# Tail of a perceiver block: output weights loaded a step sooner, query weights in four loads, products of queries and keys in four banks, and filled gaps on TensorE

## The chip, the core and the metric

The kernel runs on one NeuronCore of a Trainium2 chip. The metric is the device time of one execution in microseconds, taken as the median of several. A core has five engines that run their own instruction streams and wait for each other by semaphores: TensorE (PE), VectorE (DVE), ScalarE (ACT), GpSimd (POOL) and SyncE (SP), which here issues every transfer.

## The reference

One block over x (128 rows of 512) and a context of 12544 rows of 512, all in float32:

```
x = x + cross(layernorm(x), context)   # 16 heads of 32; q, k rms-normed; image part 257 keys, text part the rest; two softmaxes
x = x + attn(layernorm(x))             # 16 heads of 128; wq, wk, wv: 512 x 2048, wo: 2048 x 512, each codes * scales per 32 rows
x = x + moe(layernorm(x))              # 32 experts (512 -> 256 -> 512, silu gate), top 4 of 32 in 2 of 4 groups, plus a shared expert
```

## The kernel before

**Main part (to about 910 us).** The context is worked through in groups of 512 keys (`GK`), one step `s` of the loop a group, NG groups in all. In a step TensorE makes keys and values of one group, scores and softmax products of the group before it, and closes the sums of the one before that. Beside it GpSimd multiplies the codes of the self-attention weights with their scales, and SyncE passes them through a DRAM buffer called `scaled`. The step ends in a drain without new keys (s = NG, NG + 1).

**Tail.** It has these stages, all with 128 rows on the partitions:

1. `last_values`: the last products with values. ACT copies them out of PSUM (`store_attention`, L888 to L892, tile `ot_sb`), TensorE transposes, DVE scales and adds (L1296, L1298).
2. Output projection of the cross attention (PE L1814): four 128x512 products of `xnt` (shown as `kb`, copied by ACT at L988 and L990) with `wo`. DVE adds x (L1399), takes mean and variance, centers (L1079, `yn`).
3. The self attention's projections. Each of q, k and v has four column blocks of 512 (index i = 0 to 11). The product is split for precision: a high part of the weights (`weight_hi`, made by ACT, `self_high`, L984), a low part (`weight_lo`, made in place by DVE, `self_low`, L1392) and high and low parts of the input (`ynt_hi`, `ynt_lo`). One block on TensorE is 12 products of 128x512: L1829, L1832, L1836, four each. DVE adds the bias (`add_bias`, L1411) and so frees the PSUM bank. Before, all twelve blocks share two banks (`ps_pj`).
4. Transposes of q and k, scores, softmax, values (L1851, L1017, L1436, L1865), then the output projection with `weight_o` (L1893, 32 instructions). DVE adds `bo_row` to x (L1420) ahead of the bias of the first value block and ahead of the maxima of the scores.
5. DVE adds (L1453) and centers; TensorE transposes; router logits (PE L1904); 34 experts (two halves of the shared one and 32), each with an `up` product (L1916, L1919, L1922), silu on ACT (L1055), gate on DVE (L1501), two transposes and a `down` product. Weights of an expert are split on ACT (L1034, L1040) and DVE (L1441, L1447).

**What sets the order.** Every engine's order is the order in which the program issues. Transfers of the tail are issued by SyncE in the order of the code after `steps(eng, step)`: query weights (4 MB), `wo` (1 MB), the two biases (each 1 MB when spread over 128 partitions), key weights, value weights, value bias, `weight_o`, `bo_row`, gate, experts. The semaphores: `e_pj` counts finished projection blocks, `e_pjb` biased ones, `e_shi` and `e_slo` high and low parts of weights, `e_ap` the output projection of the cross attention.

The first high part (i = 0) was written into 184 KB of the on-chip memory. `wo` lies at 144 KB, where the context tile `cx` lies during the main part.

Of the kernel before, what the change touches and what calls it, by code (L numbers as in the profile page):

```python
# [10 lines left out]
P = 128  # L11
D = 512
# [30 lines left out]
def program(nc, t, out):  # L43
    ctx = ExitStack()
    with ctx:
# [93 lines left out]
        NWH = 3  # L139
        weight_hi = [sb(f"weight_hi{i}", at * KB, [P, DC, D], F32R) for i, at in enumerate((184, 128, 144))]  # L140

        sq = sb("sq", 152 * KB, [P, SF])
# [96 lines left out]
        e_cm = semaphore("codes_scaled")  # L239
        e_wl = {n: semaphore(f"weight_loaded_{n}") for n in QKV + "o"}  # L240
        e_bias = {n: semaphore(f"bias_loaded_{n}") for n in QKV}
# [90 lines left out]
        def self_block(array, i):  # L332

            return array[QKV[i // NB]][:, :, :].rearrange("p (c b) f -> p b c f", b=NB)[:, i % NB]

        N_POOL = 2 + 2 + 2 + 1 + 1 + 2 + 4

# [7 lines left out]
        def _(eng):  # L345
# [52 lines left out]
            def step(eng, s, m, loop=False):  # L398
# [22 lines left out]
                if s == 0:  # L421
                    load_next(s)
                    eng.wait_ge(e_klo, GT)
                    eng.wait_ge(e_vp, GT)
                    stack(0, True)
                if 1 <= s < NG:
                    load_next(s)
                    eng.wait_ge(e_klo, s * GT + GT)
                    if score:
                        eng.wait_ge(e_qk, s * NH - NH // 2)  # L430
                    stack(0, False)
# [12 lines left out]
            eng.wait_ge(e_pp, 2 * (NG - 1) * NPOS)  # L444
            load_matrix("q")
            eng.dma_start(wo[:, :, :], wview(t["o_wt"])).then_inc(e_wo, 16)
            load_bias("q")
            load_bias("k")
            eng.wait_ge(e_kt, NG * GT)
            eng.wait_ge(e_v, NG * GT)  # L450
            eng.wait_ge(e_pv, (NG - 1) * (NH // HC))
            load_matrix("k")
            eng.wait_ge(e_qk, NG * NH)
            load_matrix("v")
            eng.wait_ge(e_pv, NG * (NH // HC))
            load_bias("v")
            eng.wait_ge(e_x1, 1)
            load_matrix("o")
# [256 lines left out]
        def _(eng):  # L715
# [113 lines left out]
            def step(eng, s, m, loop=False):  # L829
# [146 lines left out]
            def self_high(i):  # L976

                if i % NB == 0:
                    eng.wait_ge(e_wl[QKV[i // NB]], 16)
                if i == NWH - 1:  # L980
                    eng.wait_ge(e_ap, 1)
                elif i >= NWH:
                    eng.wait_ge(e_pj, i + 1 - NWH)
                eng.activation(weight_hi[i % NWH][:, :, :], self_block(weight, i), copy).then_inc(e_shi, 1)  # L984

            self_high(0)
            eng.wait_ge(e_at, 1)
# [76 lines left out]
        def _(eng):  # L1064
# [324 lines left out]
            def self_low(i):  # L1389

                eng.wait_ge(e_shi, i + 1)
                eng.tensor_tensor(self_block(weight_lo, i), self_block(weight, i), weight_hi[i % NWH][:, :, :].bitcast(F32),  # L1392
                                  ALU.subtract).then_inc(e_slo, 1)

            self_low(0)
            self_low(1)
            eng.wait_ge(e_xb, 1)
# [4 lines left out]

            center(yn[:, :], x1[:, :])

            def add_bias(n, b):
# [4 lines left out]
                eng.wait_ge(e_rs, 3)  # L1410
                eng.scalar_tensor_tensor(part, ps_pj[b % 2][:, :], rstd, part, ALU.mult, ALU.add).then_inc(e_pjb, 1)  # L1411
# [105 lines left out]
        def _(eng):  # L1517
# [298 lines left out]


            eng.wait_ge(e_ln, 1)
            transposes(ps_t, yn).then_inc(e_lnt, 1)
            eng.wait_ge(e_lntc, 1)  # L1820

            def project(n, b):
                i = QKV.index(n) * NB + b
                high, low = weight_hi[i % NWH], self_block(weight_lo, i)
                if i >= 2:
                    eng.wait_ge(e_pjb, i - 1)
                eng.wait_ge(e_shi, i + 1)
                for c in range(DC):
                    eng.matmul(ps_pj[b % 2][:, :], ynt_hi[:, c * P:(c + 1) * P], high[:, c, :], start=(c == 0), stop=False)  # L1829
                eng.wait_ge(e_slo, i + 1)  # L1830
                for c in range(DC):
                    eng.matmul(ps_pj[b % 2][:, :], ynt_hi[:, c * P:(c + 1) * P], low[:, c, :], start=False, stop=False)  # L1832
                if i == 0:
                    eng.wait_ge(e_ylo, 1)
                for c in range(DC):
                    last = eng.matmul(ps_pj[b % 2][:, :], ynt_lo[:, c * P:(c + 1) * P], high[:, c, :], start=False, stop=(c == DC - 1))  # L1836
                last.then_inc(e_pj, 1)
# [57 lines left out]


            eng.wait_ge(e_ln, 2)
            transposes(ps_t, x3).then_inc(e_lnt, 1)
# [102 lines left out]
```

## Time and profile before

| | us |
|---|---|
| median of 3 runs | 1187.23 (1186.8 to 1187.3) |
| profiled execution, its own time | 1185.77 |
| its span, first to last instruction | 1184.0 |
| mean granted TensorE clock | 0.993 of full speed |
| PE busy / DVE busy / ACT busy / POOL busy | 1149.0 / 970.4 / 874.6 / 761.1 |

The span is what the trace shows; 1.8 us lie around it. Times in the trace count from the span's start. "Busy" is the time in which an engine executes at least one instruction, waits not counted. Each waiting instruction has in brackets how long its engine stood idle and what released it.

### The profile page before, as it was taken

How to read it: one execution, taken by the hardware profiler on the slowest of the kernel's cores; microseconds unless marked ns; L12 is line 12 of the kernel's file. 1: busy time of each engine (PE TensorE's matmuls, PEld its weight loads, DVE VectorE, ACT ScalarE, POOL GpSimd, SP SyncE). 2: the span in 40 equal slices, each digit the busy share in tenths (PEclk: the TensorE clock that was granted, in tenths of full speed). 3: DMA queues.
4: the chain of work that ended last, by engine and by line, in shares of the span. 5: the costliest groups of instructions: out<-in, count | busy, mean ns of one | idle time of the engine just before them, and what ended most of it. 6: DMA issues, size and time to landing. Idle time of an engine off the chain costs nothing.

```text
span 1184.0 us, 26319 instructions
## 1 busy us (share of the span) xinstructions
PE 1149.0 (97%) x8794; PEld 948.5 (80%) x8794; DVE 970.4 (82%) x1601; ACT 874.6 (74%) x1890; POOL 761.1 (64%) x1064
## 2 busy tenths in 40 slices
PE   6899999999999999999999999999999879999998
PEld 4778888888888888888888888888887658588886
DVE  4778888888888888888888888888887878499997
ACT  5577777778777777777777777877777756387786
POOL 6998889888888888898888988888872200000000
PEclk9999999999999999999999999999999989899999
DMA  7135776666766667766677665677655899589990
GB/s 248 46 89 140 202 194 167 182 175 177 197 179 173 186 161 198 189 178 181 167 202 193 170 180 173 178 197 179 182 144 120 257 395 398 208 300 356 367 359 12
DMA packets 129327, 236.72 MB, mean 200 GB/s; under 512 B 15014, under 2 KB 42150, under 8 KB 128812
## 3 DMA queue, kind: packets, MB, share of 16 engines
q1 hardware_dynamic: 129196, 235.05, 67.1%
q8 instruction: 73, 1.20, 0.4%
q14 instruction: 58, 0.48, 0.1%
HBM read 140.87 MB, written 17.04 MB: 133 GB/s over the span
## 4 chain that ended last, share of the span: by engine, by line
PE 91%; DMA 2%; POOL 2%; SPq 2%; DVE 1%; ACT 1%; issue 1%; DVEq 0%; ACTq 0%; POOLq 0%
PE ps L1657 39%; PE ps L1521 19%; PE ps L1684 7%; PE ps L1714 7%; PE ps L1916 3%; PE ps L1919 3%; PE ps L1922 3%; DMA wo<-o_wt 1%; SPq L361 1%; PE ps L1937 1%; PE ps L1945 1%; PE ps L1941 1%; PE ps L1893 1%; PE ps L1832 1%; PE ps L1836 1%; PE ps L1829 1%
## 5 line engine op out<-in xcount | busy, mean ns | idle before, releaser
L1657 PE MATMUL ps<-w_text,cx_blocks 128*128 128x512 f32 x1974 | 488.2, 394 | 0.5 <-ACT v_first L827 0.5
L1657 PEld LDWEIGHTS ps<-w_text,cx_blocks 128*128 128x128 f32 x1974 | 366.9, 188 | 87.0 <-issue 9.4
L873 ACT ACTIVATE p<-ps,small 128x512 f32<-128x512 f32 (+2 forms) x400 | 272.2, 681 | 142.2 <-DVE small L1234 134.7
L1232 DVE TENSOR_REDUCE small<-ps 128x1 f32<-128x512 f32 (+2 forms) x384 | 258.8, 674 | 65.0 <-PE ps L1684 61.4
L1521 PE MATMUL ps<-ident,p 128*128 128x128 f32 x1584 | 207.9, 273 | 4.5 <-DVE pt L1226 2.3
L1521 PEld LDWEIGHTS ps<-ident,p 128*128 128x128 f32 x1584 | 184.1, 140 | 34.8 <-issue 7.4
L1234 DVE TENSOR_TENSOR small<-small 128x1 f32<-128x1 f32 x384 | 164.8, 429 | 13.2
L632 POOL TENSOR_TENSOR cx_blocks<-cx_sum,small 128x256 fp32r<-128x256 f32 x188 | 119.0, 633 | 87.7 <-PE ps L1657 74.0
L851 ACT ACTIVATE pt<-ps 128x512 f32<-128x512 f32 (+1 forms) x294 | 163.2, 590 | 10.8 <-PE ps L1521 10.4
L634 POOL TENSOR_TENSOR cx_blocks<-cx_sum,cx_blocks 128x256 fp32r<-128x256 f32 x188 | 147.1, 782 | 14.7
L1684 PE MATMUL ps<-k_stack,q_stack 96*128 96x512 f32 (+1 forms) x400 | 141.8, 434 | 0.7 <-DMA k_stack<-kt_hi 0.6
L1226 DVE COPY pt<-ps 128x512 f32<-128x512 f32 (+1 forms) x106 | 72.3, 683 | 38.4 <-PE ps L1521 38.0
L770 ACT ACTIVATE squares<-kb 128x512 f32<-128x512 f32 x99 | 62.5, 632 | 43.5 <-DVE kb L1198 38.1
L1441 DVE TENSOR_TENSOR w_lo<-expert,w_hi 128x2048 fp32r<-128x2048 f32 x34 | 77.8, 2291 | 12.0 <-ACT w_hi L1034 11.9
L525 POOL TENSOR_TENSOR codes<-codes,code_scale 128x512 f32<-128x512 f32 x64 | 82.4, 1288 | 6.0 <-DMA code_scale<-code_scales 5.8
L873 ACT ACTIVATION_READ_ACCUMULATOR p<-ps,small 128x1 f32 x400 | 78.4, 196 | 0.0
L776 ACT ACTIVATE kb<-kb,small 128x512 f32<-128x512 f32 x99 | 71.2, 719 | 6.2 <-POOL small L517 6.2
L1119 DVE TENSOR_TENSOR kt_lo<-ps,kt_hi 128x512 fp32r<-128x512 f32 x99 | 67.4, 681 | 8.2 <-ACT kt_hi L781 8.2
L1034 ACT ACTIVATE w_hi<-expert 128x2048 fp32r<-128x2048 f32 x34 | 65.1, 1917 | 0.0
L625 POOL TENSOR_TENSOR cx_blocks<-cx,cx_blocks 128x512 fp32r<-128x512 f32 x47 | 60.5, 1287 | 6.7
L1714 PE MATMUL ps<-pt,v_first 128*32 128x128 f32 x1600 | 63.3, 276 | 1.0 <-ACT pt L851 0.5
L1684 PEld LDWEIGHTS ps<-k_stack,q_stack 96*128 96x128 f32 x400 | 61.4, 191 | 3.2 <-DMA k_stack<-kt_hi 1.2
(259 smaller groups left out, 1904.5 us busy)
## 6 DMA issues: line engine op xcount, KB each, us to landing
expert<-experts SPq DMA_DIRECT2D x34, 1536.0 KB, 8.6
k_stack<-kt_hi SPq DMA_DIRECT2D x384, 128.0 KB, 2.5
cx<-ctx_t SPq DMA_DIRECT2D x48, 512.0 KB, 5.1
k_stack<-kt_lo SPq DMA_DIRECT2D x192, 128.0 KB, 2.5
codes<-codes SPq DMA_DIRECT2D x64, 256.0 KB, 3.2
code_scale<-code_scales SPq DMA_DIRECT2D x64, 256.0 KB, 4.1
scaled<-codes SPq DMA_DIRECT2D x64, 256.0 KB, 2.3
weight_q<-scaled SPq DMA_DIRECT2D x1, 4096.0 KB, 15.4
```

The costliest lines, as they stand in the source:

```text
L525: eng.tensor_tensor(codes[b][:, :], codes[b][:, :], code_scale[:, :], ALU.mult).then_inc(e_cm, 1)
L632: eng.tensor_tensor(block(i, 0), of, ones.broadcast_to((P, CD, P)), ALU.mult).then_inc(e_ahi, 1)
L634: eng.tensor_tensor(block(i, 1), of, block(i, 0).bitcast(F32), ALU.subtract).then_inc(e_ab, 1)
L851: eng.activation(pt_sb[hp % NPT][:, 0:n], ps_pt[hp % 2][:, 0:n], copy).then_inc(e_pta, 1)
L873: eng.activation(pb[:, lo:hi], score_bank(s, h)[:, lo:hi], exp, bias=(ngm if g == NG - 1 else nm[1 - par])[:, col:col + 1], accum_out=ls[1 ...
L1232: eng.tensor_reduce(ngm[:, h:h + 1], score_bank(s, h)[:, lo:hi], AX.X, ALU.max, negate=True).then_inc(e_gm, 1)
L1234: eng.tensor_tensor(nm[1 - par][:, h:h + 1], ngm[:, h:h + 1], old[:, h:h + 1], ALU.min).then_inc(e_nm, 1)
L1441: eng.tensor_tensor(w13_lo[n % 2][:, :, :], slot[n % NR][:, 0:DC, :], w13_hi[n % 2][:, :, :].bitcast(F32), ALU.subtract).then_inc(e_13lo, 1)
L1521: last = eng.transpose(dst[:, c * P:(c + 1) * P], src[:, c * P:(c + 1) * P], ident[:, :])
L1657: last = eng.matmul(ps_a[(p + i + 1) % 2][:, :], blk[:, i, a, c * P:(c + 1) * P], w_t[:, i, w, c * D:(c + 1) * D], start=(i in FRESH and c ...
L1684: eng.matmul(score_bank(s, h)[:, 0:n], q_st[qi][0:NST * HD, head, :], stk[0:NST * HD, head, 0:n], start=True, stop=True).then_inc(e_qk, 1)
L1714: last = eng.matmul(into[jp * HD:(jp + 1) * HD, :], vb[k][:, head * HD:(head + 1) * HD], pt_sb[[head_at(gp, x) for x in range(NH)].index(h ...
```

## The change

- The load of `wo` moves from the tail into step s = NG - 1, behind a wait for the last block split on GpSimd (`e_ab`), when the tile below it is free.
- The load of the query weights is issued as four loads, one for each column block, each with its own semaphore. Key weights are issued ahead of the two biases. `weight_o` waits for the first projected block (`e_pj` 1) and not for x after the cross attention (`e_x1`), since a new tile `first_weight_hi` lies in its place.
- ACT makes the high part of block 0 in two halves, into that new tile: one ahead of the last copy of `ot_sb`, the other after it.
- DVE makes the low part of block 1 after the centering and no longer ahead of the addition of x; the low part of block 3 comes ahead of the first bias.
- The eight blocks of q and k go round four PSUM banks; those of v use two.
- TensorE gets 16 transposes of the identity into an unused bank at each of two places where it waits for DVE's centering (`fill`).

```
@@ SyncE @@
                     stack(0, True)
+                if s == NG - 1:
+                    eng.wait_ge(e_ab, 2 * (NG - 1) * NPOS)
+                    eng.dma_start(wo[:, :, :], wview(t["o_wt"])).then_inc(e_wo, 16)
                 if 1 <= s < NG:
...
             eng.wait_ge(e_pp, 2 * (NG - 1) * NPOS)
-            load_matrix("q")
-            eng.dma_start(wo[:, :, :], wview(t["o_wt"])).then_inc(e_wo, 16)
-            load_bias("q")
-            load_bias("k")
+            def load_query_block(b):
+                eng.dma_start(self_block(weight, b), scaled[0:NWT].rearrange("(c b) p f -> p b c f", b=NB)[:, b]).then_inc(e_wlq[b], 16)
+            load_query_block(0)
+            for b in range(1, NB):
+                load_query_block(b)
...
             load_matrix("k")
+            load_bias("q")
+            load_bias("k")
             eng.wait_ge(e_qk, NG * NH)
             load_matrix("v")
             eng.wait_ge(e_pv, NG * (NH // HC))
             load_bias("v")
-            eng.wait_ge(e_x1, 1)
+            eng.wait_ge(e_pj, 1)
             load_matrix("o")
@@ all engines @@
+        first_hi = sb("first_weight_hi", 112 * KB, [P, DC, D], F32R)
+        def bank_of(i):
+            return (*ps_pj, *ps_sc[0:2])[i % NB] if i < 2 * NB else ps_pj[i % 2]
+        def high_of(i):
+            return weight_hi[i % NWH] if i else first_hi
@@ ScalarE @@
                     store(g - 1, 15)
+                    eng.wait_ge(e_wlq[0], 16)
+                    eng.activation(first_hi[:, 0:CD, :], self_block(weight, 0)[:, 0:CD, :], copy)
                     store_attention(1)
...
-                if i % NB == 0:
+                if i < NB:
+                    eng.wait_ge(e_wlq[i], 16)
+                elif i % NB == 0:
                     eng.wait_ge(e_wl[QKV[i // NB]], 16)
                 if i == NWH - 1:
                     eng.wait_ge(e_ap, 1)
-                elif i >= NWH:
+                elif i > NWH:
                     eng.wait_ge(e_pj, i + 1 - NWH)
...
-            self_high(0)
+            eng.activation(first_hi[:, CD:, :], self_block(weight, 0)[:, CD:, :], copy).then_inc(e_shi, 1)
@@ VectorE @@
             self_low(0)
-            self_low(1)
...
             center(yn[:, :], x1[:, :])
+            self_low(1)
...
             self_low(2)
+            self_low(3)
             for i in range(2 * NB):
                 add_bias(QKV[i // NB], i % NB)
-                self_low(i + NWH)
+                if i + NB < 3 * NB - 1:
+                    self_low(i + NB)
@@ TensorE @@
+            def fill(n):
+                for _ in range(n):
+                    eng.transpose(ps[7][:, 0:P], ident[:, :], ident[:, :])
+            fill(16)
             eng.wait_ge(e_ln, 1)
             transposes(ps_t, yn).then_inc(e_lnt, 1)
...
-                if i >= 2:
-                    eng.wait_ge(e_pjb, i - 1)
+                if i >= NB:
+                    eng.wait_ge(e_pjb, i - 3 if i < 2 * NB + 2 else i - 1)
...
+            fill(16)
             eng.wait_ge(e_ln, 2)
             transposes(ps_t, x3).then_inc(e_lnt, 1)
```

How the order moves, at three places. First SyncE, the end of the main part and the start of the tail, of before:

```order
L411 DMA o_rows<-v_img_b 128x512
L361 DMA k_stack<-kt_hi 32x2x512 [waits scores,kt_lo]
...
L413 DMA x_again<-x 128x512
L439 DMA weight_q<-scaled 128x16x512 [waits product_done]
L446 DMA wo<-o_wt 128x4x512
L442 DMA sq<-bq 128x2048
L442 DMA sk<-bk 128x2048
L439 DMA weight_k<-scaled 128x16x512 [waits pv_batch,v_stored,k_transposed]
L439 DMA weight_v<-scaled 128x16x512 [waits scores]
L442 DMA sv<-bv 128x2048 [waits pv_batch]
L439 DMA weight_o<-scaled 128x16x512 [waits x_after_cross]
L459 DMA bo_row<-bo 128x512
```

and of the change:

```order
L419 DMA o_rows<-v_img_b 128x512
L436 DMA wo<-o_wt 128x4x512 [waits block_split]
L369 DMA k_stack<-kt_hi 32x2x512 [waits scores,kt_lo]
...
L457 DMA weight_q<-scaled 128x4x512 [waits product_done]
L457 DMA weight_q<-scaled 128x4x512 x3
L450 DMA weight_k<-scaled 128x16x512 [waits pv_batch,v_stored,k_transposed]
L453 DMA sq<-bq 128x2048
L453 DMA sk<-bk 128x2048
L450 DMA weight_v<-scaled 128x16x512 [waits scores]
L453 DMA sv<-bv 128x2048 [waits pv_batch]
L450 DMA weight_o<-scaled 128x16x512 [waits self_projected]
L474 DMA bo_row<-bo 128x512
```

`wo` has left the row of loads of the tail and stands ahead of the last step's 24 transfers of `k_stack`; from the query weights to `bo_row` the row is otherwise the same, with the key weights ahead of two biases.

Second VectorE, from the low part of block 0 to the first biases (`weight_lo_q` is a low part, `sq` a bias), of before:

```order
L1392 TENSOR_TENSOR weight_lo_q<-weight_q,weight_hi_140 128x4x512 [waits self_weight_hi]
L1392 TENSOR_TENSOR weight_lo_q<-weight_q,weight_hi_141 128x4x512 [waits self_weight_hi]
L1399 TENSOR_TENSOR x_149<-ps,x_again 128x512 [waits attention_projected,x_again_biased]
...
L1079 TENSOR_SCALAR yn<-x_149,small 128x512 [waits variance]
L1414 TENSOR_TENSOR ynt_lo<-ps,ynt_hi 128x512 [waits normed_t_stored]
L1392 TENSOR_TENSOR weight_lo_q<-weight_q,weight_hi_142 128x4x512 [waits self_weight_hi]
L1411 SCALAR_TENSOR_TENSOR sq<-ps,small,sq 128x512 [waits rsqrt,self_projected,bias_loaded_q]
```

and of the change:

```order
L1411 TENSOR_TENSOR weight_lo_q<-weight_q,first_weight_hi 128x4x512 [waits self_weight_hi]
L1417 TENSOR_TENSOR x_150<-ps,x_again 128x512 [waits attention_projected,x_again_biased]
...
L1098 TENSOR_SCALAR yn<-x_150,small 128x512 [waits variance]
L1411 TENSOR_TENSOR weight_lo_q<-weight_q,weight_hi_141 128x4x512 [waits self_weight_hi]
L1433 TENSOR_TENSOR ynt_lo<-ps,ynt_hi 128x512 [waits normed_t_stored]
L1411 TENSOR_TENSOR weight_lo_q<-weight_q,weight_hi_142 128x4x512 [waits self_weight_hi]
L1411 TENSOR_TENSOR weight_lo_q<-weight_q,weight_hi_140 128x4x512 [waits self_weight_hi]
L1430 SCALAR_TENSOR_TENSOR sq<-ps,small,sq 128x512 [waits rsqrt,self_projected,bias_loaded_q]
```

One low part now stands between the centering and `ynt_lo`, and a second one ahead of the first bias.

Third TensorE, from the output projection to the first block, in the change:

```order
L1835 MATMUL ps<-wo,kb_98 128x512 [waits attention_t_stored,wo_loaded]
L1835 MATMUL ps<-wo,kb_98 128x512 [waits attention_t_stored] x3
L1842 MATMUL ps<-ident 128x128 x16
L1542 MATMUL ps<-ident,yn 128x128 [waits normed]
L1542 MATMUL ps<-ident,yn 128x128 x3
L1856 MATMUL ps<-first_weight_hi,ynt_hi 128x512 [waits self_weight_hi,normed_t_stored]
```

The 16 transposes of the fill (L1842) wait for nothing and stand where TensorE waited for `yn`; the same row is new ahead of the transposes of `x3`.

## Rows read from the trace of the kernel before

**Rows 1.** The page, part 1: busy us (share of the span) x instructions, of all engines

```profile
PE 1149.0 (97%) x8794; PEld 948.5 (80%) x8794; DVE 970.4 (82%) x1601; ACT 874.6 (74%) x1890; POOL 761.1 (64%) x1064
```

**Rows 2.** The chain that ended last, 930 to 1040 us: start us, us, what

```profile
933.95 17.62 DMA wo<-o_wt
951.61 5.27 PE ps L1814 x8
...
968.85 0.91 PE ps L1832 x4
...
990.35 0.87 PE ps L1521 x8
...
1009.72 13.75 PE ps L1893 x32
```

**Rows 3.** DMA issues from 880 us on: each one's KB, median us to landing

```profile
weight_q<-scaled SPq DMA_DIRECT2D x1, 4096.0 KB, 15.4
...
weight_v<-scaled SPq DMA_DIRECT2D x1, 4096.0 KB, 35.5
...
wo<-o_wt SPq DMA_DIRECT2D x1, 1024.0 KB, 17.6
...
bo_row<-bo SPq DMA_DIRECT2D x1, 256.0 KB, 22.3
```

**Rows 4.** Timeline of SyncE: start us, us, engine line op out<-in [idle before <-releaser]

```profile
901.71 0.43 SPq L411 DMA_DIRECT2D o_rows<-v_img_b  x1
...
933.45 0.45 SPq L439 DMA_DIRECT2D weight_q<-scaled  x1
...
942.68 15.83 SPq L439 DMA_DIRECT2D weight_v<-scaled  x1
...
969.94 12.40 SPq L459 DMA_DIRECT2D bo_row<-bo  x1
```

**Rows 5.** Timeline of GpSimd, its last block split

```profile
893.01 0.75 POOL L634 TENSOR_TENSOR cx_blocks<-cx,cx_blocks 128x256 fp32r<-128x256 f32 x1
```

**Rows 6.** Timeline of ScalarE around the end of the cross attention

```profile
946.93 0.28 ACT L892 ACTIVATE ot_sb<-ps 128x128 f32<-128x128 f32 x1 [1.28 <-PE ps L1714]
948.92 1.91 ACT L984 ACTIVATE weight_hi<-weight_q 128x2048 fp32r<-128x2048 f32 x1 [1.70 <-DMA weight_q<-scaled]
```

**Rows 7.** Timeline of VectorE, the addition of `bo_row`

```profile
992.32 0.69 DVE L1420 TENSOR_TENSOR x<-x,bo_row 128x512 f32<-128x512 f32 x1 [1.37 <-DMA bo_row<-bo]
```

**Rows 8.** Timeline of TensorE at its waits for DVE and ACT

```profile
959.21 0.66 PE L1521 MATMUL ps<-ident,yn 128*128 128x128 f32 x4 [2.35 <-DVE yn L1079]
...
1000.71 0.66 PE L1521 MATMUL ps<-ident,sq 128*128 128x128 f32 x4 [0.45 <-DVE sq L1436]
...
1025.71 0.66 PE L1521 MATMUL ps<-ident,x 128*128 128x128 f32 x4 [2.25 <-DVE x L1079]
1027.05 1.92 PE L1904 MATMUL ps<-gate_w,x3t 128*128 128x32 f32 x8 [0.69 <-ACT x3t L1045]
```

**Rows 9.** Stretches: us, busy (x) of PE, PEld, DVE, ACT, POOL; clock, DMA, GB/s

```profile
931.00:932.00 1.00, 0.82 (x4) 0.46 (x4) 1.00 (x3) 1.00 (x4) 0.00 (x0) 1.00 0.93 205
...
944.00:948.00 4.00, 2.88 (x46) 2.21 (x47) 3.58 (x10) 1.87 (x5) 0.00 (x0) 1.00 1.05 388
...
957.00:961.00 4.00, 1.10 (x6) 0.82 (x7) 2.52 (x5) 2.41 (x2) 1.14 (x6) 1.00 1.05 388
962.00:965.00 3.00, 3.00 (x8) 2.34 (x7) 1.43 (x1) 0.00 (x0) 0.00 (x0) 0.50 1.04 383
...
1027.00:1033.00 6.00, 5.95 (x18) 5.08 (x19) 3.72 (x18) 2.06 (x3) 0.00 (x0) 0.50 0.00 0
```

**Rows 10.** Tile `weight_hi`: duration ns min/median/max, first and last start us, forms

```profile
L1392 DVE TENSOR_TENSOR weight_lo_k<-weight_k,weight_hi x4: 2284/2286/2287, 970.0 to 978.6; 128x2048 fp32r<-128x2048 f32 x4
```

**Rows 11.** Timelines of ScalarE and VectorE at the start of the experts

```profile
1033.90 0.48 ACT L1055 ACTIVATE m_a<-ps,small 128x256 f32<-128x256 f32 x1 [3.31 <-PE ps L1922]
...
1036.22 2.29 DVE L1441 TENSOR_TENSOR w_lo<-expert,w_hi 128x2048 fp32r<-128x2048 f32 x1 [0.96 <-ACT w_hi L1034]
```

More of the change, by code:

```diff
@@ L239, in program @@
         e_cm = semaphore("codes_scaled")
-        e_wl = {n: semaphore(f"weight_loaded_{n}") for n in QKV + "o"}
+        e_wl = {n: semaphore(f"weight_loaded_{n}") for n in "kvo"}
+        e_wlq = [semaphore(f"weight_loaded_q{b}") for b in range(NB)]
         e_bias = {n: semaphore(f"bias_loaded_{n}") for n in QKV}
@@ L981, in self_high @@
                     eng.wait_ge(e_ap, 1)
-                elif i >= NWH:
+                elif i > NWH:
                     eng.wait_ge(e_pj, i + 1 - NWH)
-                eng.activation(weight_hi[i % NWH][:, :, :], self_block(weight, i), copy).then_inc(e_shi, 1)
-            self_high(0)
+                eng.activation(high_of(i)[:, :, :], self_block(weight, i), copy).then_inc(e_shi, 1)
+            eng.activation(first_hi[:, CD:, :], self_block(weight, 0)[:, CD:, :], copy).then_inc(e_shi, 1)
             eng.wait_ge(e_at, 1)
@@ L1391, in self_low @@
                 eng.wait_ge(e_shi, i + 1)
-                eng.tensor_tensor(self_block(weight_lo, i), self_block(weight, i), weight_hi[i % NWH][:, :, :].bitcast(F32),
+                eng.tensor_tensor(self_block(weight_lo, i), self_block(weight, i), high_of(i)[:, :, :].bitcast(F32),
                                   ALU.subtract).then_inc(e_slo, 1)
             self_low(0)
-            self_low(1)
             eng.wait_ge(e_xb, 1)
@@ L1410, in add_bias @@
                 eng.wait_ge(e_rs, 3)
-                eng.scalar_tensor_tensor(part, ps_pj[b % 2][:, :], rstd, part, ALU.mult, ALU.add).then_inc(e_pjb, 1)
+                eng.scalar_tensor_tensor(part, bank_of(NB * QKV.index(n) + b)[:, :], rstd, part, ALU.mult, ALU.add).then_inc(e_pjb, 1)
             eng.wait_ge(e_lntc, 1)
@@ L1823, in project @@
                 i = QKV.index(n) * NB + b
-                high, low = weight_hi[i % NWH], self_block(weight_lo, i)
-                if i >= 2:
-                    eng.wait_ge(e_pjb, i - 1)
+                high, low = high_of(i), self_block(weight_lo, i)
+                if i >= NB:
+                    eng.wait_ge(e_pjb, i - 3 if i < 2 * NB + 2 else i - 1)
                 eng.wait_ge(e_shi, i + 1)
                 for c in range(DC):
-                    eng.matmul(ps_pj[b % 2][:, :], ynt_hi[:, c * P:(c + 1) * P], high[:, c, :], start=(c == 0), stop=False)
+                    eng.matmul(bank_of(i)[:, :], ynt_hi[:, c * P:(c + 1) * P], high[:, c, :], start=(c == 0), stop=False)
                 eng.wait_ge(e_slo, i + 1)
                 for c in range(DC):
-                    eng.matmul(ps_pj[b % 2][:, :], ynt_hi[:, c * P:(c + 1) * P], low[:, c, :], start=False, stop=False)
+                    eng.matmul(bank_of(i)[:, :], ynt_hi[:, c * P:(c + 1) * P], low[:, c, :], start=False, stop=False)
                 if i == 0:
@@ L1835, in project @@
                 for c in range(DC):
-                    last = eng.matmul(ps_pj[b % 2][:, :], ynt_lo[:, c * P:(c + 1) * P], high[:, c, :], start=False, stop=(c == DC - 1))
+                    last = eng.matmul(bank_of(i)[:, :], ynt_lo[:, c * P:(c + 1) * P], high[:, c, :], start=False, stop=(c == DC - 1))
                 last.then_inc(e_pj, 1)
```

## The prediction

> **What bounds the kernel now.** I read the page first: TensorE is busy 97% of the span [rows 1], so until about 910 us, and again in the steady run of the experts, nothing but TensorE's own work counts, and the change touches neither. What is left is the tail between 930 and 1040 us. Its chain [rows 2] leaves TensorE for the load of `wo` until 951.6; TensorE also waits for DVE at 959.21, 1000.71 and 1025.71 [rows 8].
>
> Then I read the loads. Issue plus time to landing [rows 3, 4] gives: query weights 933.45 + 15.4 = 948.9; `wo` 933.95 + 17.6 = 951.6 [rows 2]; value weights 942.68 + 35.5 = 978.2; `bo_row` 969.94 + 22.3 = 992.2. They land in the order of issue: the 1 MB of `wo` comes 2.7 us behind the query weights, and at that pace two biases, key and value weights (10 MB) would land 27.0 us after `wo`, at 978.6, where the row says 978.2. So it is one stream without a gap, at 383 to 388 GB/s [rows 9]. DVE stands at `bo_row` until 992.32, released by that very load [rows 7]. From there it runs without a wait (sum, bias of the first value block, four maxima, a low part, a bias, the first normed rows), and TensorE transposes them at 1000.71, after only 0.45 us of idle [rows 8]. **The stream of loads sets the end** of this stage; TensorE's own chain is half a microsecond behind it.
>
> The third thing is TensorE's granted clock. With 1.10 us of work between 957 and 961 it fell to 0.50 (1.2 GHz) in 962 to 965; after the second centering it was 0.50 in 1027 to 1033 [rows 9].
>
> **The change part by part.**
>
> `wo` a step sooner. It is issued after `o_rows` (901.71) [rows 4]; the wait in front of it is for the last block split, over at 893.8 [rows 5], so it holds nothing up, and the transfers of `k_stack` behind it in the queue come later, with the last keys. Effect 1: the output projection starts when its input is there. ACT's last copy of `ot_sb` ends at 947.2 [rows 6]; the second half of block 0's high part takes 1 us (half of 1.91), then the two copies follow: 949.0 and not 951.6. Effect 2: the stream is 1 MB shorter from the query weights on, so all behind them lands **2.7 us** sooner: value weights 975.5, `bo_row` 989.5.
>
> Query weights in four loads: the same bytes. Block 0 is there after a quarter, about 941.5, and ACT wants it at 945.65. The half high part (1 us) fits into ACT's wait of 1.28 us for the last value product [rows 6]. Cost 0; with the cover gone, 1 us.
>
> Key weights ahead of the biases: key weights land at 948.9 + 10.8 = 959.7, the query bias at 962.4. With two banks TensorE would now stand before block 2, as the first block is done near 959; with four, the first bias is wanted when block 4 starts, at 967. Cost 0.
>
> TensorE's new chain: output projection 949.0 to 952.5 at full clock (5.27 us before, part of it at half clock [rows 2]), centering 2.35 us as before [rows 8], first product at 956.1. A block is three times 0.91 us [rows 2]; the query blocks end at 967, the key blocks at 979.5. DVE's low part takes 2.29 us, and one with a bias 2.86 (four starts from 970.0 to 978.6) [rows 10]; that keeps pace. The low part now ahead of `ynt_lo` ends at 957.0 and `ynt_lo` at 957.7, just before TensorE wants it, at 957.9. This chain is 6 us earlier, and then it meets the stream: value weights at 975.5, high part 977.5, low part 979.7, two rounds of 2.86 and a bias of 0.66: the last key bias is done at 986.1, and DVE waits for `bo_row` until 989.5. **Of the 6 us only the 2.7 of the stream are kept.** The fixed 8.4 us of DVE (992.32 to 1000.71) then lead to the first transposes at 998.0.
>
> A new wait grows there. TensorE goes on at 986.2 with 4 transposes (0.44 us), scores (32 small products, 3.5 us at the pace of rows 2) and two value blocks (5.5 us), is done at 995.6 to 996, and stands still for 2.0 to 2.4 us where it stood 0.45. The wait itself costs nothing, but the clock may fall: it did with 2.35 us and 0.69 us of idle [rows 8, 9]. The third value block (2.73 us), whose bias is on the way to the last normed rows, would take up to 1.7 us longer, since the half-clock row shows at least 3 us of it. Bounds 0 and 1.7. That rests on where the fall lands, which need not be the same in every execution; I take 0.7.
>
> `weight_o` behind the first finished block: that one ends at 958.9, and SyncE comes to this load only when its queue takes it (969.3 before, just ahead of `bo_row`). Cost 0.
>
> Fills: 8 transposes take 0.87 us [rows 2], 16 take 1.75, less than the waits of 2.35 and 2.25 us in which they stand. Cost 0; at half clock they would take 3.5 us and push what follows by 1.2 us each, but both start behind work at full clock. What the first holds is hidden by the stream. The second decides the start of the experts. At half clock the logits took 1.92 us [rows 8]; now 0.96 to 1.92. The router on DVE follows them, so the first gate comes 0 to 0.96 sooner. The first `up` (12 products) takes 2.7 us and not 4.9, so silu starts near 1030.8 (counted without the 2.7 above) and not at 1033.9, and ACT's next high part, for which DVE waited 0.96 us until 1036.22 [rows 11], is ready in time. DVE's low part starts 0.96 + 0.96 = **1.9 us** sooner. Bounds: 2.2 if the steps behind it gain a little too, 0 if the clock falls all the same.
>
> Sum: 2.7 + 1.9 - 0.7 = 3.9 us. The profiled execution took 1185.77 us: 1181.9. The median of the runs is 1.46 us above it, and I apply the sum to that: 1187.23 - 3.9 = **1183.3 us**.
>
> **Two rules weighed.** In 944 to 948 TensorE was busy 2.88 of 4 us, transposes among the work, and its clock stayed 1.00 [rows 9]; I take it that transposes hold it. The Trainium skill, "TensorE: Matmul & The Clock Gate", section Part 4: PE-mode transpose, says that full clock doesn't engage for them, as they don't count as busy in the same way. By that rule the fills do nothing.
>
> 1 MB behind another load costs 2.7 us [rows 2, 3]. The Trainium skill, "DMA: Bandwidth & Descriptors", section Bandwidth, gives 6.15 us for 1 MB by itself; four such would make 24.6 us of the query weights, an estimate from that figure. The trace disagrees for loads in a row.
>
> **The rivals.**
>
> *The clock falls at the new wait in every execution, in full.* For it: the wait is as long as the one that brought a fall. Against: only one idle, dense products around it. 2.7 + 1.9 - 1.7 = 2.9: 1184.3. Chance 0.17.
>
> *The fills don't hold the clock.* Behind the second, idles of 0.5 and 0.69 us and logits products of 32 columns remain. 2.7 - 0.7 = 2.0: 1185.2, and 1186.2 with the full 1.7. Chance 0.18. The Trainium skill's rule on transposes, above, would give this time.
>
> *The stream gets slower, and so the kernel.* Just ahead of the query weights the 128 KB transfers of `k_stack` moved 205 GB/s [rows 9]. If the four loads, with their stride, ran like that, they would take 20.5 us and not 10.8, all behind them would land 9.7 - 2.7 = 7.0 us later than before: 1187.23 + 7.0 - 1.9 = 1192.3. The kernel is slower from 4.6 us more on these 4 MB, below some 270 GB/s. Against: the 2 KB pieces are the same as before. Chance 0.04.
>
> *DVE does not wait for `bo_row`.* If the stream is faster than 2.7 us suggests, more of the 6 us comes through, at most all: 1187.23 - 6.0 - 1.9 = 1179.3. Against: value weights bind ahead of it. Chance 0.08.
>
> *The moved load does not free the stream*, since something else paces it, such as SyncE's issue: only the fill's 1.9 is left, less 0.7: 1186.0. Against: 383 GB/s and more throughout. Chance 0.05.
>
> **The numbers.** Forecast 0.48, the others as above. About 0.2%, 2.4 us, is what a measurement of this kernel can tell from no change, so "faster" is below 1184.9. There lie the forecast, the first rival, a third of the second, and the fourth: 0.48 + 0.17 + 0.06 + 0.08 = 0.79. Same 0.17, slower 0.04. The range runs from 1181.2 (no fall, 2.2 at the experts, and a little of the fourth rival) to 1186.1 (fills and clock lost).
>
> **What would show it.** Right: the output projection starts at 949 behind ACT and takes 3.5 us; DVE waits some 3 us for `bo_row`, until 989.5; L1893 starts 2 to 2.7 us sooner; the clock is 1.00 from 1020 to 1040; the experts' steady run comes 3.9 us sooner. Wrong: no wait at `bo_row`; value weights later than 976; half clock in the first `up`; ACT waiting for block 0 ahead of its copy of `ot_sb`.

## The result and the profile after

| | before | this kernel |
|---|---|---|
| median, us | 1186.34 (10 runs, 1184.4 to 1187.3) | 1180.72 (9 runs, 1177.4 to 1183.9) |
| ratio, 95% interval | | 0.995 [0.9941, 0.996]: 5.9 us less, 4.7 to 7.0 |
| profiled execution, its span | 1185.77, 1184.0 | 1179.77, 1178.0 |
| 930 to 1040 us: TensorE busy, clock | 97.1, 0.94 | 100.5, 1.00 |

One execution of this kernel took 6545 us, for a reason that the record doesn't show, and is left out. The kernel is faster by 0.5%. Its median lies below the forecast (1183.3) by 2.6 us and below the range (from 1181.2) by 0.5. About 0.9 us of that is the starting point: the forecast counted from 1187.23, the median of 3 runs, and the ten runs gave 1186.34. The rest is the gain itself, 5.9 us by the ratio and 6.0 by the two profiles, where the sum had 3.9.

The load stream first. SyncE's timeline after, to hold against [rows 4]:

```profile
903.18 0.43 SPq L436 DMA_DIRECT2D wo<-o_wt  x1
...
933.54 2.13 SPq L457 DMA_DIRECT2D weight_q<-scaled  x4
935.78 2.60 SPq L450 DMA_DIRECT2D weight_k<-scaled  x1
938.42 11.46 SPq L453 DMA_DIRECT2D sq<-bq  x1
...
966.17 12.39 SPq L474 DMA_DIRECT2D bo_row<-bo  x1
```

The page's part on DMA issues after (KB each, median us to landing), to hold against [rows 3]:

```profile
weight_v<-scaled SPq DMA_DIRECT2D x1, 4096.0 KB, 24.0
...
wo<-o_wt SPq DMA_DIRECT2D x1, 1024.0 KB, 7.7
...
bo_row<-bo SPq DMA_DIRECT2D x1, 256.0 KB, 22.5
```

`wo` is there at 910.9. The query weights are issued when they were before (933.54 against 933.45). `bo_row` lands at 988.7, where I forecast 989.5 and where it was 992.3. VectorE's timeline shows the wait for it, now 2.83 us long [rows 7]:

```profile
988.72 0.69 DVE L1441 TENSOR_TENSOR x<-x,bo_row 128x512 f32<-128x512 f32 x1 [2.83 <-DMA bo_row<-bo]
```

The chain that ended last, after (start us, us, what), to hold against [rows 2]: it now runs from the queue over this load.

```profile
966.17 22.53 DMA bo_row<-bo
988.72 0.70 DVE x L1441
989.45 0.75 DVE sv L1430
...
996.36 0.70 DVE sq L1457
997.11 0.66 PE ps L1542 x4
```

TensorE's timeline after, its waits of the tail that the prediction spoke of and the one at the last key bias, to hold against [rows 8]:

```profile
949.11 3.67 PE L1835 MATMUL ps<-wo,kb 128*128 128x512 f32 x8 [0.36 <-ACT kb L1007]
...
955.13 0.66 PE L1542 MATMUL ps<-ident,yn 128*128 128x128 f32 x4 [0.60 <-DVE yn L1098]
...
985.95 0.66 PE L1542 MATMUL ps<-ident,sk 128*128 128x128 f32 x4 [0.88 <-DVE sk L1430]
...
997.11 0.66 PE L1542 MATMUL ps<-ident,sq 128*128 128x128 f32 x4 [1.45 <-DVE sq L1457]
...
1022.11 0.66 PE L1542 MATMUL ps<-ident,x 128*128 128x128 f32 x4 [0.50 <-DVE x L1098]
1023.46 1.08 PE L1932 MATMUL ps<-gate_w,x3t 128*128 128x32 f32 x8 [0.69 <-ACT x3t L1064]
```

The output projection starts behind ACT, at 949.1, and the softmax transposes are 3.6 us sooner, exactly as much as `bo_row`. The fourth row is the new wait, 1.45 us. The stretches after (columns as in [rows 9]) show that the clock (third number from the end) stayed at its full level, 2.4 GHz, where it had been 1.2 GHz:

```profile
962.00:965.00 3.00, 3.00 (x15) 2.49 (x14) 1.64 (x3) 1.92 (x1) 0.00 (x0) 1.00 1.05 392
...
1027.00:1033.00 6.00, 5.29 (x24) 3.88 (x23) 5.45 (x20) 4.86 (x6) 0.00 (x0) 1.00 0.00 0
```

Timelines of ScalarE and VectorE at the start of the experts, to hold against [rows 11]: the first silu comes 6.4 us sooner, the low part 5.5 us and without a wait.

```profile
1027.49 0.47 ACT L1074 ACTIVATE m_a<-ps,small 128x256 f32<-128x256 f32 x1 [1.33 <-PE ps L1950]
...
1030.75 2.28 DVE L1462 TENSOR_TENSOR w_lo<-expert,w_hi 128x2048 fp32r<-128x2048 f32 x1
```

### The profile page after: what moved, and what is told of

Read it like the earlier page. It is cut to its first block, busy times and chain, and to the rows that moved or that the text cites. A ratio compares the mean times of both kernels' runs of the same rounds, so it can differ in the third digit from the quotient of the medians.

```text
span 1178.0 us, 26386 instructions
## 1 busy us (share of the span) xinstructions
PE 1148.5 (97%) x8826; PEld 948.3 (80%) x8826; DVE 969.9 (82%) x1601; ACT 874.2 (74%) x1891; POOL 763.5 (65%) x1064
## 4 chain that ended last, share of the span: by engine, by line
PE 80%; SPq 8%; DMA 4%; POOL 3%; DVE 2%; issue 1%; ACT 1%; ACTq 0%; POOLq 0%; DVEq 0%
PE ps L1678 35%; PE ps L1542 17%; PE ps L1705 7%; PE ps L1735 7%; SPq L369 4%; PE ps L1944 3%; PE ps L1947 2%; PE ps L1950 2%; SPq L453 2%; DMA bo_row<-bo 2%; PE ps L1965 1%; PE ps L1973 1%; PE ps L1969 1%; PE ps L1920 1%; DMA k_stack<-kt_hi 1%
## 5 line engine op out<-in xcount | busy, mean ns | idle before, releaser
L1251 DVE TENSOR_REDUCE small<-ps 128x1 f32<-128x512 f32 (+2 forms) x384 | 258.8, 674 | 61.8 <-PE ps L1705 57.9
L1253 DVE TENSOR_TENSOR small<-small 128x1 f32<-128x1 f32 x384 | 160.7, 419 | 13.2
L796 ACT ACTIVATE kt_hi<-ps 128x512 fp32r<-128x512 f32 x99 | 59.1, 597 | 10.5 <-DMA k_stack<-kt_hi 9.6
```

The costliest lines, as they stand in the source:

```text
L1251: eng.tensor_reduce(ngm[:, h:h + 1], score_bank(s, h)[:, lo:hi], AX.X, ALU.max, negate=True).then_inc(e_gm, 1)
L1253: eng.tensor_tensor(nm[1 - par][:, h:h + 1], ngm[:, h:h + 1], old[:, h:h + 1], ALU.min).then_inc(e_nm, 1)
```

## The measure used for the experiments

The same code ahead of the tail doesn't take the same time in every execution: the query weights were issued between 930.95 and 935.10 us in the profiled executions of the 17 kernels here. A difference of two spans is uncertain by that much, so I count from this issue and cut what follows in three. **Stage**: to the start of the router's logits (in which the landing of `bo_row` is shown too). **Start of the experts**: from there to the third `m_h` (the gated product that DVE writes once for each expert). **Experts**: from the third `m_h` to the last. Each comes from the start times in the timelines, in us.

| kernel | `bo_row` lands | stage | start of experts | experts | ratio of the times to before [95%] |
|---|---|---|---|---|---|
| before | 58.9 | 93.6 | 16.95 | 133.1 | 1 |
| the change | 55.2 | 89.9 | 15.0 | 132.6 | 0.9950 [0.9941, 0.9960] |
| e1 no second fill | 55.2 | 89.9 | 15.6 | 132.5 | 0.9955 [0.9943, 0.9967] |
| e2 no first fill | 55.3 | 90.0 | 15.1 | 132.5 | 0.9963 [0.9951, 0.9975] |
| e9 neither fill | 55.2 | 90.5 | 16.3 | 132.5 | 0.9959 [0.9946, 0.9973] |
| e3 one query load | 56.3 | 92.3 | 15.0 | 132.6 | 0.9972 [0.9961, 0.9982] |
| e4 `wo` in the stream | 59.4 | 94.1 | 15.0 | 132.6 | 0.9975 [0.9967, 0.9984] |
| e13 the same | 58.1 | 92.8 | 15.0 | 132.6 | one time |
| e14 `wo` and biases | 58.1 | 92.8 | 15.0 | 133.2 | one time |
| e7 biases first | 55.5 | 90.2 | 15.0 | 132.6 | 0.9956 [0.9944, 0.9968] |
| e11 two banks | 55.2 | 94.6 | 15.6 | 132.6 | 0.9991 [0.9982, 1.0000] |
| e5 before, `wo` early | 56.1 | 91.1 | 15.6 | 133.2 | 0.9987 [0.9974, 1.0000] |
| e8 before, fills | 58.5 | 93.2 | 15.0 | 132.6 | 0.9980 [0.9968, 0.9992] |
| e10 before, four loads | 57.9 | 93.2 | 17.1 | 132.6 | 0.9994 [0.9982, 1.0006] |
| e6 `bo_row` early | | 88.3 | 15.7 | 132.5 | 0.9945 [0.9927, 0.9964] |
| e12 and five more fills | | 88.2 | 15.0 | 132.6 | 0.9932 [0.9919, 0.9945] |
| e15 and key bias first | | 87.1 | 15.0 | 132.6 | 0.9941 [0.9926, 0.9956] |

0.001 of the ratio is 1.2 us. The first four columns are from one execution each, the last from 5 to 12. By this measure the change is worth 3.7 + 1.9 + 0.5 = 6.1 us.

## The experiments

### The stream: one query load, `wo` back in it

e3 puts one 4 MB load in place of the four; all blocks then wait for it:

```diff
-            load_query_block(0)
-            for b in range(1, NB):
-                load_query_block(b)
+            eng.dma_start(weight["q"][:, :, :], scaled[0:NWT].rearrange("i p f -> p i f")).then_inc(e_wlq[0], 16)
```

> The changed kernel with the query weights in one load of 4 MB again. The stream came 3.6 us sooner where 1 MB less makes 2.7; the missing 0.9 lies in its first 6 us (935 to 941: 2.0 MB before, 2.35 MB now). Theory A (four loads of a quarter start faster than one of 4 MB): 935 to 941 moves some 2.0 MB again, bo_row lands at 989.6, the time is 0.9 us more than the change's. Theory B (the start is faster for another reason, such as wo being out of the queue, or by chance): 2.35 MB, bo_row 988.7, the time as the change's, 6.0 less than before. In both, ACT waits for block 0 until 948, the output projection starts near 951 instead of 949.1, hidden by the stream.

Theory A holds. These are the 8 us behind the issue of the query weights, the last number is GB/s. Before:

```profile
933.45:941.45 8.00, 6.96 (x97) 5.18 (x95) 6.27 (x11) 6.09 (x16) 1.29 (x1) 1.00 0.97 310
```

The change:

```profile
933.54:941.54 8.00, 6.95 (x97) 5.18 (x95) 6.29 (x11) 6.12 (x16) 1.29 (x1) 1.00 0.98 352
```

e3:

```profile
932.40:940.40 8.00, 6.65 (x94) 4.99 (x93) 5.99 (x11) 5.81 (x16) 1.28 (x1) 1.00 0.97 308
```

e10, the kernel before with four loads:

```profile
930.95:938.95 8.00, 7.53 (x102) 5.79 (x100) 6.88 (x12) 6.67 (x18) 1.28 (x1) 1.00 0.98 356
```

One load of 4 MB starts at about 310, four of 1 MB at 352 to 356; 42 GB/s for 8 us is 0.34 MB, 0.9 us at 386. The other profiles agree: 321 in e5 and 327 in e8, which have one load, and 347 to 358 in all thirteen with four. The rest of my expectation was wrong: the late block 0 isn't hidden. ScalarE's timeline of e3:

```profile
947.92 1.06 ACT L971 ACTIVATE first_weight_hi<-weight_q 128x1024 fp32r<-128x1024 f32 x1 [3.34 <-DMA weight_q<-scaled]
```

ACT waits 3.34 us for the load, TensorE's first product comes 26.9 us behind the issue and not 22.9, and TensorE no longer stands before the softmax transposes: its chain is now the later one. The stage is 2.3 us longer, and the time 2.6 us by the ratios (0.9 to 4.3).

> The kernel before, with the query weights in four loads, nothing else. Theory (four loads start faster than one of 4 MB, whatever lies behind them): the first 8 us behind their issue move 2.8 MB and not 2.48, wo and all behind it lands 0.9 us sooner, bo_row 58.0 us behind the issue and not 58.9; the output projection, which waits for wo, 0.9 us sooner too; time 0.9 us less than before, if the clock falls in the same places. Rival (wo behind the query weights eats it, as bo_row came 59.4 us behind the issue in the changed kernel with wo in the stream): bo_row at 58.9 or later, time as before.

`bo_row` came at 57.9, by the theory, but the stage gained only 0.4 us: the clock was 0.50 from 956 to 962, from the transposes of `yn` into the second query block, and TensorE's own chain was last. The time, 0.7 us less, can't be told from none. In these profiles four loads pay with an earlier TensorE only.

e4 moves the load of `wo` back behind the last query block.

> The changed kernel with wo loaded behind the query weights again, all else as in the change. Theory (the stream): everything behind wo lands 2.7 us later, bo_row at 991.4, DVE released by it, the time 2.7 us more than the change's, 3.3 less than before. If wo in the queue is also what slowed the start of the stream (935 to 941), 3.6 us more. Rival (the moved load does not shorten the stream, something else paces it): bo_row at 988.7 and the time as the change's.

The stage was 4.2 us longer, more than the theory, and the timing says 3.0. This size stayed open, so two more runs went to it: e13, the same kernel, and e14, which moves the two biases in front of the key weights as well.

> The same edit as e4_wo_in_stream, a second look. There bo_row landed 59.4 us behind the issue of the query weights, 4.2 more than without wo, where 1 MB makes 2.7. If that was chance of one execution: 57.9 to 58.1 now, and the softmax transposes 2.7 us later than in the change counted from that issue. If it belongs to this order of loads: 59.4 again.

> The changed kernel with wo and the two biases in the places they had before, so the order of loads of before with four query loads, as in e10_before_four_loads (57.9 there). Theory (bytes alone count, 2.7 us for each MB): bo_row 57.9 us behind the issue of the query weights. Rival (wo ahead of the 4 MB of key weights without the biases between them costs more): 57.9 here and 59.4 in e13; or 59.4 in both if it is the changed kernel's other work.

Both gave 58.1. So 59.4 was one execution's, and **1 MB costs 58.1 - 55.2 = 2.9 us**; e5 below, against the kernel before, gives 2.7. e7 changes the order of the biases alone:

> The changed kernel with the query and key biases ahead of the key weights again. Theory (only the end of the stream counts, and its bytes are the same): bo_row lands 55.2 us behind the issue of the query weights as in the change; the key weights land 5.4 us later, ACT and TensorE wait some 2 us for them, the last key bias on DVE comes 2 us later and its wait for bo_row shrinks from 2.8 us to 0.8 or less; the time is as the change's within 0.5 us. Rival (the biases, 128 rows from one row of memory, move at another rate in this place, so that the order changes the stream): bo_row lands over 0.5 us sooner or later than 55.2.

55.5 and 0.7 us more time than the change, inside the uncertainty. No cost of the order is seen. But DVE's wait for `bo_row` stayed 2.83 us, so the key weights had more room than I gave them.

### `wo` early alone

> The kernel before, with wo alone a step sooner. Theory (stream and TensorE's own chain both end near 1000, and the change shortened both): the stream is 2.6 us shorter, bo_row lands 56.2 us behind the issue of the query weights and not 58.9; but the query weights still land 15.4 us behind theirs, ACT still splits block 0 before its copies, so the output projection starts as late as before and TensorE's chain is no sooner; it gains the 0.45 us it was idle before the softmax transposes. Time 0.4 to 0.5 us less than before. Rival (the stream alone set the end): 2.6 to 2.7 us less than before. The run also shows whether the experts' pace of 4.354 us per expert, against 4.333 in all five kernels with the change, is this code's.

The stream came 2.7 us sooner as expected, and so did the stage, by 2.5, as the rival had it; my 0.45 was wrong. Between the output projection and the logits TensorE's clock stayed 1.00, where it was 0.50 for 3.4 us before [rows 9], and that gave TensorE's chain what it lacked. The timing, 1.5 us less (0 to 3.1), lies between. The profiled execution was the fastest of the twelve, and its mean granted clock the highest: 0.995, against 0.988 to 0.994 in the other eleven. So most of them had more time at half clock; where it lay isn't shown.

### The fills

Each is `fill(16)` left out, or in e8 added to the kernel before.

> The changed kernel without the 16 transposes ahead of the wait for the third normed rows. Theory (the stream of loads sets the end of the first stage, the second fill keeps the clock for the start of the experts): nothing moves before 1019; bo_row lands at 988.7; the clock falls to 0.50 for some 6 us between 1022 and 1030, the logits take 1.9 us and not 1.08, DVE's first w_lo with a late high part starts 1.9 us later than with the fill. Time: 1.9 us more than the change, that is 3.7 to 4.1 us less than before. Rival (the fill holds nothing, the clock at 1020 to 1033 is owed to the work ahead of the wait coming sooner): clock 1.00 there all the same, time as the change, 6.0 us less than before.

> The changed kernel without the 16 transposes ahead of the wait for the first centering. Theory (this stage ends with the stream of loads): the clock falls to 0.50 for some 3.5 us from about 958 on, the query blocks end some 1.7 us later, but bo_row still lands at 988.7 and releases DVE, whose wait for it shrinks from 2.8 us to some 1.1; the time is as the change's, 6.0 us less than before, within 0.3. Rival (the end of this stage was TensorE's own chain, which the fill shortened): DVE no longer waits for bo_row and the time is 1.5 to 3 us more than the change's.

> The changed kernel without either group of transposes. Without the first alone the clock stayed 1.00 from 940 to 1040, without the second alone it fell once, for 3.4 us from 1022 on, and the third m_h came 0.6 us later. Theory (the first does nothing for the time, the second is worth 0.6 to 1.9 us by the place and length of the fall): bo_row and the softmax transposes as in the change, one fall in 1021 to 1033, time 0.6 to 1.9 us more than the change's. Rival (the fills are worth nothing): clock 1.00, time as the change's.

> The kernel before, with the two groups of 16 transposes alone. Theory as predicted (the second keeps the clock from falling in 1026 to 1033): the logits take 1.08 us and not 1.92, the third m_h comes 15.0 us behind the logits and not 17.0, time 1.9 us less than before; the first one can add at most the 0.45 us by which TensorE's chain is behind DVE. Rival (the fall costs 0.6 us in most executions, as in the changed kernel without the second fill, and 1.9 in some): 0.5 to 1.0 us less than before.

Stretches at the start of the experts, the clock third from the end. e1:

```profile
1023.00:1027.00 4.00, 4.00 (x14) 3.11 (x14) 3.35 (x21) 1.15 (x3) 0.00 (x0) 0.70 0.00 0
```

e9:

```profile
1023.00:1027.00 4.00, 4.00 (x13) 3.42 (x14) 2.45 (x11) 1.57 (x2) 0.00 (x0) 0.50 0.00 0
```

e8:

```profile
1024.00:1033.00 9.00, 7.62 (x38) 5.95 (x37) 6.43 (x28) 6.07 (x8) 0.41 (x2) 1.00 0.00 0
```

Over all profiles: without the second fill (before, e1, e5, e9, e10) the clock fell there in five of five, and the start of the experts took 15.6 to 17.1 us; with it, it fell in two of twelve (e6, e11: 15.7 and 15.6), and took 15.0 to 15.1 in the others. So the second fill is worth 0.6 to 2.1 us, by where the fall lands. e8 has both fills added to the kernel before: 1.95 us less in the start of the experts, 2.4 us less in the time (0.9 to 3.8). The clocks of all executions bear it out: the mean granted clock of e8's twelve was 0.991 to 0.997, with 0.995 in the middle, and that of the 29 of the kernel before beside them 0.988 to 0.995, with 0.991 in the middle. In the changed kernel the timings are too wide to show a fill: against the change, e1 takes 0.6 us more, e9 1.1 and e2 1.5, and each difference is uncertain by nearly 2 us. Without the first fill the clock stayed 1.00 in e2, fell for 3.4 us in e9, and `bo_row` landed at 55.2 to 55.3 in both. DVE's wait for it took the loss, 1.04 us in e9 and not 2.83. The 0.5 us more in e9's stage come from half clock at the transposes of `x3`.

### Two banks

```diff
-            return (*ps_pj, *ps_sc[0:2])[i % NB] if i < 2 * NB else ps_pj[i % 2]
+            return ps_pj[i % 2]
```

and the wait for the banks in `project` as it was before.

> The changed kernel with the query and key products in two banks again. Theory: TensorE now stands before the third query block until the query bias has landed and the first bias is added, 0.1 to 0.4 us, and a few tenths at each of the next; some 1 us in all on TensorE's chain, hidden by DVE's wait for bo_row, 2.8 us, which shrinks by as much; bo_row 55.2 us behind the issue of the query weights, time as the change's within 0.3 us. Rival (the banks were a part of the gain): the wait for bo_row gone and 1 us or more above the change.

The rival, and far beyond it: the stage is 4.7 us longer, the time 4.9 us by the ratios (3.3 to 6.4). The wait for `bo_row` is gone. TensorE's timeline of e11:

```profile
963.34 1.20 PE L1856 MATMUL ps<-weight_hi,ynt_hi 128*128 128x512 f32 x4 [0.79 <-DVE sq L1430]
967.61 1.20 PE L1856 MATMUL ps<-weight_hi,ynt_hi 128*128 128x512 f32 x4 [1.25 <-DVE sq L1430]
971.36 1.21 PE L1856 MATMUL ps<-weight_hi,ynt_hi 128*128 128x512 f32 x4 [0.72 <-DVE sq L1430]
975.62 1.20 PE L1856 MATMUL ps<-weight_hi,ynt_hi 128*128 128x512 f32 x4 [0.77 <-DVE sq L1430]
979.41 1.19 PE L1856 MATMUL ps<-weight_hi,ynt_hi 128*128 128x512 f32 x4 [0.33 <-DVE sk L1430]
983.70 1.21 PE L1856 MATMUL ps<-weight_hi,ynt_hi 128*128 128x512 f32 x4 [0.83 <-DVE sk L1430]
```

and VectorE's, behind one of these waits:

```profile
968.35 2.29 DVE L1411 TENSOR_TENSOR weight_lo_k<-weight_k,weight_hi 128x2048 fp32r<-128x2048 f32 x1 [0.79 <-ACT weight_hi L1003]
970.55 0.75 DVE L1430 SCALAR_TENSOR_TENSOR sq<-ps,small,sq 128x512 f32<-128x512 f32 x1
972.62 2.29 DVE L1411 TENSOR_TENSOR weight_lo_k<-weight_k,weight_hi 128x2048 fp32r<-128x2048 f32 x1 [1.31 <-ACT weight_hi L1003]
```

Here is a loop that I didn't see. The bank comes free with a bias, which stands on DVE behind a low part of 2.29 us; the low part waits for ACT's high part, that waits for a finished product, and the product for its bank. I had counted only the first turn of it. The six waits make 4.7 us. From the first product to the last key transposes TensorE takes 35.8 us and not 29.5, 6.4 more; the stage grows by less, since the 1.45 us in which TensorE waited before the softmax transposes are used up first. What the order of DVE's work (the late first bias) adds to the two banks wasn't tried, nor were ACT's two halves of block 0 and the moved low parts tried by themselves.

### What bounds the changed kernel: `bo_row`, then TensorE

e6 moves one line of the load queue:

```diff
             eng.wait_ge(e_pv, NG * (NH // HC))
+            eng.dma_start(bo_row[:, :], rows_of(t["bo"])).then_inc(e_bo, 16)
             load_bias("v")
...
-            eng.dma_start(bo_row[:, :], rows_of(t["bo"])).then_inc(e_bo, 16)
```

> The changed kernel with bo_row loaded ahead of the value bias, right behind the value weights, and not behind weight_o. Theory (DVE's wait for bo_row sets the end of the stage): the wait of 2.8 us is gone, TensorE's own chain is next; it is done with the second and third value block 1.4 us before it goes on now, less a few tenths, so the softmax transposes start 1.1 to 1.4 us sooner, and the time is 1.1 to 1.4 us less than the change's, 7.1 to 7.4 less than before. Rival (the value weights bind just ahead of bo_row, or something behind it does): less than 0.3 us.

TensorE's timeline of e6: the third value block, the softmax transposes and the fourth block follow each other, where the change had 1.45 us of idle time.

```profile
995.00 1.07 PE L1863 MATMUL ps<-weight_hi,ynt_lo 128*128 128x512 f32 x4
995.91 0.60 PE L1542 MATMUL ps<-ident,sq 128*128 128x128 f32 x4
996.26 1.18 PE L1856 MATMUL ps<-weight_hi,ynt_hi 128*128 128x512 f32 x4
```

The stage is 1.6 us shorter. In this execution the clock fell 1.6 us behind the start of the logits, which gave 0.7 back, and the time (0.9945) can't be told from the change's. e12 adds `fill(5)` behind the transposes of `x3`:

> bo_row ahead of the value bias, and five more transposes of the identity behind those of x3, in the 0.69 us in which TensorE waits for ACT's copy ahead of the logits. Theory (with bo_row early the clock fell once, 1.3 us behind the start of the logits, and cost 0.66 us; more work in the waits keeps it): clock 1.00 from 940 to 1040, third m_h 15.0 us behind the logits, time 1.6 us less than the change's, 7.5 less than before. Rival (five more hold nothing, where the fall lands is chance): third m_h 15.6 to 17 us behind the logits, and the time 0.5 to 1.0 us less than the change's.

It kept the clock at 1.00, and is **8.1 us faster than before** (6.5 to 9.6), 2.1 more than the change by point estimates, uncertain by 1.9. One profile doesn't show that it was the five that held it: with the second fill the clock held in ten of twelve, e12 and e15 among them.

```diff
-                add_bias(QKV[i // NB], i % NB)
+                if i < 2 * NB - 1:
+                    add_bias(QKV[i // NB], i % NB)
+                if i == 2 * NB - 2:
+                    add_bias("k", NB - 1)
                 if i + NB < 3 * NB - 1:
                     self_low(i + NB)
```

> On top of e12_bo_early_more_fill: DVE adds the last key bias before it makes the low part of the third value block, not behind it. Theory (with bo_row early TensorE's chain sets the end of the stage, with 0.89 us in it of waiting for that bias): the wait is gone, the softmax transposes come 0.9 us sooner counted from the issue of the query weights, the time is 0.9 us less than e12's, 8.9 less than before. Rival (DVE, which then has the low part in the way of the sum with bo_row and the maxima, is next): less than 0.3 us.

TensorE's stop of 0.89 us before the last key transposes is gone and the stage is 1.1 us shorter, so TensorE's chain was the bound. Its timing does not repeat it: 7.0 us less than before (5.2 to 8.8), an interval that overlaps e12's. The profiled execution was the fastest of its five, with a mean clock of 0.999 where the other four had 0.997 and 0.998 (e12's five had 0.998 and 0.999), so half clock that the profile doesn't show may be in it. Which of the two is faster stays open. Both beat the kernel before; that e15 beats the change isn't shown.

## Why the prediction was too high

The sum missed 2.1 us of the profiles' 6.0: 0.9 in the stream, 0.7 in the clock, 0.5 in the experts. Step by step:

**What bounds the tail: right.** `bo_row`'s load released DVE, all behind it moved by as much as it (3.6 us), and of TensorE's earlier chain only this came through. Taking `bo_row` away as the bound (e6) gave 1.6 us at once.

**The stream, 2.7 us forecast, 3.6 in the profile: here the prediction failed.** The term for `wo` was sound: 1 MB was 2.7 us (e5) to 2.9 (e13 and e14 against the change). The step that failed is "Query weights in four loads: the same bytes", with cost 0: it took equal bytes for equal time, and four loads bring all behind them 0.9 to 1.1 us sooner (e3, e10). 4 MB took 15.4 us [rows 3], which is 272 GB/s from issue to landing, where the queue gave 388 afterwards [rows 9]; a slow start stood in the rows, and I took it for fixed. The rival of a slower stream looked at the same place, with the wrong sign. The half high part did fit into ACT's wait, as forecast (output projection at 949.1). But what block 0 after a quarter of the load is worth had no price: with one load TensorE starts 4 us later, is the later chain, and the stage is 2.3 us longer (e3).

**The clock at the new wait, -0.7 us: this term failed too, none of it was seen.** The wait was 1.45 us and not 2.0 to 2.4, since the stream was faster than I had it, and the clock was 1.00 from 985 to 1010 in all 17 profiles. The rival that it falls there every time is out.

**The second fill, 1.9 us: right** in this pair of profiles (16.95 - 15.04), by luck in its exact size: in others it was a third of it to all. "The fills don't hold the clock" is out: five falls in five without, two in twelve with. The Trainium skill, "TensorE: Matmul & The Clock Gate", section Part 4: PE-mode transpose, by whose rule the fills do nothing, is contradicted by these rows for the transposes of this kernel: in e8 they were all that was added, and the clock was 1.00 where it was 0.50 [rows 9].

**Left over: 0.5 us in the experts**, which the sum didn't have. It isn't the change's: from the third to the last `m_h` took 132.5 to 132.6 us in 14 profiles and 133.1 to 133.2 in three, among them e14, which is the changed kernel with three loads moved. So 3.6 + 1.9 + 0.5 = 6.0 us, and 0.5 of it is the pair of profiles. That the medians differ by as much, 5.9, is in part luck too: the profiled execution of before had a mean clock of 0.993, and 58 of 83 others of the same kernel, timed beside the experiments, had 0.991 or less.

**Four banks: cost 0 was right, their worth wasn't weighed.** "With four, the first bias is wanted when block 4 starts" is right as far as it goes; but with two, and DVE's new order, little of the rest shows (e11: 0.9991, 1.1 us less than before, 0 to 2.1). **Key weights ahead of the biases: 0, right** (e7).

The range was too narrow at its low end. It reached 6.0 us below its starting point, by no fall, 2.2 us at the experts and a little of the rival of a faster stream, which had 0.08. A stream 0.9 us faster and no fall already make 5.5 with the 1.9 of the fill.

## What to carry to other kernels

When a stage ends with a stream of loads, compute each load's rate from the profile, its first microseconds too: a start at 310 GB/s in a queue that runs at 386 is a term of its own. Buffers that let one engine run ahead may cost nothing and show no gain in their own place, and still carry most of a change: follow the loop engine by engine for more than one turn. And before a wait is charged or credited, look which chain is second: here TensorE's was ready 1.5 us before the stream let it go on, so each part of the change was worth what the other left it.

## What the runs showed of the hardware

- One load of 4 MB moved 308 to 327 GB/s in its first 8 us (four profiles: before, e3, e5, e8), four of 1 MB 347 to 358 (thirteen), with the same 2 KB pieces and other loads behind them. Why, no run tells.
- Behind the same wait, the one for the third normed rows, half clock began at 1020.6 in e9, before the logits (1022.4), and at 1022.0 in e1, behind their start (1020.9). That is the difference between 16.3 and 15.6 us, with the same code from the first query product on in both.
- In three of 17 profiles the experts took 0.5 us more from the third `m_h` to the last. Between 1065 and 1170 us one expert took 4.354 us in the kernel before and 4.333 in the change, with TensorE never idle in either.
- The kernel before took 1180.9 to 1189.1 us in 29 executions beside e5, e6, e8 and e9, and the issue of the query weights varies by 4 us between profiles, under code ahead of it that differs in nothing but the place of `wo`'s load. A part goes with the granted clock: of 83 executions of the kernel before beside the experiments, the 25 with a mean clock of 0.993 or more took 1184.5 us on average, the 41 with 0.990 or less 1186.3. What sets the rest was not followed up.
